# Attention on one core: pairs of key steps with one narrow group each, and maxima over 512 keys

## The reference

```python
h = _sln(hidden, w, ln_g, ln_b, Wg, bg, Wb, bb)
qkv = (h @ Wqkv.T + bqkv).reshape(B, N, num_heads, hd, 3)
...
energy = jnp.einsum('bhqd,bhkd->bhqk', q, k)
att = jax.nn.softmax(energy, axis=-1) / D ** 0.5
out = jnp.einsum('bhqk,bhkd->bhqd', att, v)
```

## Time and profile before

| | us |
|---|---|
| median of 3 runs | 1984.32 (1983.32 to 1984.5) |
| the profiled execution | 1984.56 |
| its span, first to last instruction | 1982.8 |
| TensorE busy | 1898.3 (96%) |
| VectorE busy | 1208.9 (61%) |
| GpSimd busy | 1147.7 (58%) |
| ScalarE busy | 809.0 (41%) |

### The profile page before, as it was taken

The page is one execution under the profiler, slowest core; times in us unless marked ns, Lnnn a source line. Parts: engine busy times, 40 slices in busy tenths (PEclk is TensorE's granted clock), DMA queues, the critical chain, the costliest instruction groups (busy, mean ns, idle before and its releaser), DMA issues. The chain is left out here.

```text
span 1982.8 us, 28225 instructions
## 1 busy us (share of the span) xinstructions
PE 1898.3 (96%) x10520; PEld 1242.2 (63%) x10520; DVE 1208.9 (61%) x1510; ACT 809.0 (41%) x1373; POOL 1147.7 (58%) x589
## 2 busy tenths in 40 slices
PE   6699999999998999998999999999999999999995
PEld 1478888888886888885455555555555555454584
DVE  3556555555646545445766666666666666664289
ACT  1332123122212222211466666666666666666300
POOL 0565565566445121122477777777777777777545
PEclk9899999999999999997899999999999999999997
DMA  6301010100113464566344323444443234405293
GB/s 240 125 1 54 30 56 21 53 32 21 53 40 136 155 215 169 189 197 190 84 98 103 85 78 78 101 108 98 108 103 88 78 78 99 107 24 182 99 391 121
DMA packets 117688, 212.47 MB, mean 107 GB/s; under 512 B 18598, under 2 KB 36134, under 8 KB 117576
## 3 DMA queue, kind: packets, MB, share of 16 engines
q1 hardware_dynamic: 98828, 200.04, 34.1%
q10 hardware_dynamic: 18560, 10.94, 1.9%
q0 software_dynamic: 192, 0.05, 0.0%
HBM read 134.40 MB, written 75.80 MB: 106 GB/s over the span
## 5 line engine op out<-in xcount | busy, mean ns | idle before, releaser
L1371 DVE TENSOR_REDUCE at_mrow<-banks 128x1 f32<-128x1024 f32 x512 | 604.3, 1217 | 270.5 <-PE banks L1204 270.4
L1349 ACT ACTIVATE at_probs<-banks 128x512 f32<-128x512 f32 x1024 | 557.3, 597 | 324.8 <-PE banks L1220 323.7
L1468 POOL TENSOR_TENSOR at_pair<-at_probs 128x2048 f32<-128x2048 f32 x127 | 581.8, 4581 | 170.4 <-ACT at_probs L1349 170.4
L1220 PE MATMUL banks<-early_qs,early_ks 98*128 98x512 f32 x1024 | 442.6, 435 | 5.5 <-ACT at_probs L1349 5.5
L1204 PE MATMUL banks<-early_ks,early_qs 96*128 96x512 f32 x1024 | 375.9, 412 | 6.7 <-PEq L754 3.5
L1220 PEld LDWEIGHTS banks<-early_qs,early_ks 98*128 98x128 f32 x1024 | 191.8, 188 | 211.4 <-ACT at_probs L1349 109.9
L1232 PE MATMUL banks<-at_probs,at_v 128*32 128x512 f32 x2048 | 273.0, 605 | 0.9 <-ACT at_probs L1349 0.9
L1204 PEld LDWEIGHTS banks<-early_ks,early_qs 96*128 96x128 f32 x1024 | 198.2, 196 | 45.3 <-DVE at_mrow L1371 18.8
L67 PE MATMUL banks<-l_ht,l_weights 128*128 128x512 f32 x768 | 179.4, 393 | 5.5 <-ACT l_gt L574 5.5
L67 PE MATMUL banks<-qk_nt,l_weights 128*128 128x512 f32 x768 | 177.2, 392 | 3.0 <-ACT qk_gt L889 3.0
L67 PE MATMUL banks<-l_weights,l_hf 128*128 128x512 f32 x768 | 177.3, 390 | 0.0
(11 more groups left out here) (120 smaller groups left out, 1988.1 us busy)
## 6 DMA issues: line engine op xcount, KB each, us to landing
qk_scratch<-qk_out SPq DMA_DIRECT2D x64, 512.0 KB, 2.8
early_ks<-qk_scratch SPq DMA_DIRECT2D x48, 512.0 KB, 7.0
early_qs<-qk_scratch SPq DMA_DIRECT2D x96, 256.0 KB, 11.6
attn_scratch<-at_out SPq DMA_DIRECT2D x32, 512.0 KB, 2.6
o_a<-attn_scratch SPq DMA_DIRECT2D x32, 512.0 KB, 11.3
v_scratch<-qk_v ACTq DMA_DIRECT2D x32, 256.0 KB, 2.4
at_v<-v_scratch SPq DMA_DIRECT2D x16, 512.0 KB, 14.0
o_x<-x_scratch SPq DMA_DIRECT2D x8, 1024.0 KB, 14.2
```

Of the source, the lines that this page charges most:

```text
L1220: pe.matmul(et[j % 2][:], ks[0:98, slot, j, (i % KC) * P:(i % KC + 1) * P], qs[0:98, slot, i // KC, j, :], start=True, stop=True).then_inc ...
L1349: nc.scalar.activation(probs[:, i % 4, j, :], et[j % 2][:], ACT.Exp).then_inc(exp_done, 1)
L1371: nc.vector.tensor_reduce(mrow[:, half, u:u + 1], e_ps[u % 2], AX.XY, ALU.max).then_inc(max_done, 1)
L1468: nc.gpsimd.tensor_tensor(psum2[:, pair % 2], probs[:, a], probs[:, a + 1], ALU.add).then_inc(pair_ready, 1)
```

## The change

Two steps form a pair, and the pair becomes the unit of every order.

- On TensorE, `FRONT` puts 8 energy products and 8 products for the maxima of a pair into one sequence, then come both `av` and one whole `den`, that of the pair before. At the head of a half `den` stands between the two `av`.
- The banks are dealt out anew: three for energies, three for the maxima, one each for `av` and `den`. Maxima are taken over 512 keys, one bank at a time, so there are twice as many reductions, each half as long. `mrow` has two values per query. `turn_max` turns both with plain products by the identity into the bank of the third product that follows, and VectorE joins them with one more reduction.
- 20 units come before the first step, not 26. `SWITCH` is pair 3, and the turns stand in pairs 2 and 6.
- ScalarE copies `av` and `den` out behind the last exponential of a step, and `den` of the previous group behind step 1 (it was step 3).
- VectorE's reciprocal of the previous group's second half stands behind pair 1, that is step 3 (it was step 5).
- SP spreads those denominators before it stores the first half, and widens the reciprocal before it places the negated maxima.

The diff, cut:

```diff
-        LEAD = 13
-        SWITCH = STEPS - LEAD
-        TURN = (SWITCH + KC + 1, SWITCH + 1)
+        LEAD = 5
+        SWITCH = PAIRS - LEAD
+        TURN = (SWITCH + PAIRS // 2 - 1, SWITCH - 1)
+        SPAN = PAIRS // QH
+        FRONT = ("M", "E") * 6 + ("E", "M", "E", "M")
         PARTS = 2
         DC = CH // PARTS
-        DEN_STEP = KC // 2 - 1
...
-        mrow = sb("at_mrow", [P, QH, UNITS])
+        mrow = sb("at_mrow", [P, QH, 2, UNITS])
...
-        et = sh.ps[0:2]
-        e_ps = [sh.psum[:, 2:4], sh.psum[:, 4:6]]
+        et, em = sh.ps[0:3], sh.ps[3:6]
...
+        def units_of_pair(g, slot, p, with_next):
+            if p >= SWITCH and not with_next:
                 return []
...
-        FIRST_UNITS = 2 * LEAD
+            whose, at = (g + 1, (slot + 1) % RING) if p >= SWITCH else (g, slot)
+            n = 4 * ((p - SWITCH) % PAIRS)
+            return [(whose, at, (n + a) // UNITS, (n + a) % UNITS, keys) for a in range(4) for keys in range(2)]
+        def number(g, half, u, keys):
+            return 2 * (UNITS * (QH * g + half) + u) + keys
+        def turn_bank(g, half):
+            return den_ps if g == 0 and half == 0 else em[(2 * UNITS * halves(g, half) + 2) % 3]
+        FIRST_UNITS = 4 * LEAD
...
+                    spread_den(g - 1, 1)
                     store(g - 1, 0)
-                    spread_den(g - 1, 1)
+                    widen_rden(g - 1, 1)
                 place_neg(g, slot, 1)
+                spread_den(g, 0)
                 if not first:
-                    widen_rden(g - 1, 1)
                     store(g - 1, 1)
-                spread_den(g, 0)
+                widen_rden(g, 0)
                 if with_next:
                     place_neg(g + 1, (slot + 1) % RING, 0)
-                widen_rden(g, 0)
...
-            def max_unit(unit, keys):
...
-                pe.matmul(e_ps[u % 2][:, keys, :], qs[0:96, slot, half, j, c * P:(c + 1) * P],
+            def max_unit(g, slot, half, u, keys):
+                n, j, c = number(g, half, u, keys), u // TT, u % TT
+                if n >= 3:
+                    pe.wait_ge(max_done, n - 2)
+                if n > 2 * UNITS * QH and n % (2 * UNITS) == 2:
+                    pe.wait_ge(negt_taken, n // (2 * UNITS))
+                pe.matmul(em[n % 3][:], qs[0:96, slot, half, j, c * P:(c + 1) * P],
                           ks[0:96, slot, j, keys * CH:(keys + 1) * CH], start=True, stop=True).then_inc(e_done, 1)
             def turn_max(g, half):
-                pe.wait_ge(max_done, UNITS * halves(g, half))
...
-                pe.transpose(den_ps[0:UNITS, 0:P], mrow[:, half], sh.ident[:]).then_inc(mrow_turned, 1)
+                pe.wait_ge(max_done, 2 * UNITS * halves(g, half))
+                for keys in range(2):
+                    last = pe.matmul(turn_bank(g, half)[0:UNITS, keys * P:(keys + 1) * P], mrow[:, half, keys],
+                                     sh.ident[:], start=True, stop=True)
+                last.then_inc(mrow_turned, 1)
             def energies(g, slot, i, j):
...
-                pe.matmul(et[j % 2][:], ks[0:98, slot, j, (i % KC) * P:(i % KC + 1) * P],
+                n = HG * (STEPS * g + i) + j
+                if n >= 3:
+                    pe.wait_ge(exp_done, n - 2)
+                pe.matmul(et[n % 3][:], ks[0:98, slot, j, (i % KC) * P:(i % KC + 1) * P],
                           qs[0:98, slot, i // KC, j, :], start=True, stop=True).then_inc(et_done, 1)
...
-            def den(g, pair, parts, turned=None):
+            def den(g, pair):
                 pe.wait_ge(pair_ready, PAIRS * g + pair + 1)
...
+                n = pair % SPAN
+                if n == 0:
+                    if g == 0 and pair == 0:
+                        pe.wait_ge(negt_taken, 1)
+                    else:
+                        pe.wait_ge(den_taken, QH * g + pair // SPAN)
+                for part in range(PARTS):
                     cols = slice(DC * part, DC * (part + 1))
                     for j in range(HG):
                         last = pe.matmul(den_ps[HD * j:HD * (j + 1), cols], ones_col[:], psum2[:, pair % 2, j, cols],
...
+                                         start=n == 0 and part == 0, stop=n == SPAN - 1 and part == PARTS - 1)
+                last.then_inc(den_done, 1)
+            def den_before(g, p):
+                if p > 0:
+                    den(g, p - 1)
+                elif g > 0:
+                    den(g - 1, PAIRS - 1)
...
             def group(g, slot, nth=None, first=False, load=True, with_next=True):
                 nxt = (slot + 1) % RING
...
-                for i in range(STEPS):
-                    if i % KC == 0:
-                        pe.wait_ge(negm_loaded, 32 * halves(g, i // KC))
-                    if with_next and i == SWITCH:
+                for p in range(PAIRS):
+                    if p % SPAN == 0:
+                        pe.wait_ge(negm_loaded, 32 * halves(g, p // SPAN))
+                    if with_next and p == SWITCH:
                         pe.wait_ge(stack_loaded[nxt], LOADS * (nth + 1))
...
+                    products = iter(units_of_pair(g, slot, p, with_next))
+                    e = 0
+                    for kind in FRONT:
+                        if kind == "E":
+                            energies(g, slot, 2 * p + e // HG, e % HG)
+                            e += 1
+                        else:
+                            for product in islice(products, 1):
                                 max_unit(*product)
...
+                    av(g, slot, 2 * p)
+                    if p % SPAN == 0:
+                        den_before(g, p)
+                        av(g, slot, 2 * p + 1)
+                    else:
+                        av(g, slot, 2 * p + 1)
+                        if p == TURN[1]:
+                            turn_max(g, 1)
+                        if with_next and p == TURN[0]:
+                            turn_max(g + 1, 0)
+                        den_before(g, p)
...
-                        act.wait_ge(et_done, HG * (STEPS * g + i) + j + 1)
-                        nc.scalar.activation(probs[:, i % 4, j, :], et[j % 2][:], ACT.Exp).then_inc(exp_done, 1)
-                        if j == 1 and i == KC:
...
-                        if j == 1 and i == 0 and not first:
...
-                    if i == KC // 2 - 1 and not first:
+                        n = HG * (STEPS * g + i) + j
+                        act.wait_ge(et_done, n + 1)
+                        nc.scalar.activation(probs[:, i % 4, j, :], et[n % 3][:], ACT.Exp).then_inc(exp_done, 1)
+                    if i % KC == KC - 1:
+                        take_av(g, i // KC)
+                    if i == 1 and not first:
                         take_den(g - 1, 1)
-                    if i == KC + KC // 2 - 1:
+                    if i == KC + 1:
                         take_den(g, 0)
...
-            def take_max(g, slot, half, u, n):
-                dve.wait_ge(e_done, 2 * (n + 1))
-                nc.vector.tensor_reduce(mrow[:, half, u:u + 1], e_ps[u % 2], AX.XY, ALU.max).then_inc(max_done, 1)
+            def take_max(g, slot, half, u, keys):
+                n = number(g, half, u, keys)
+                dve.wait_ge(e_done, n + 1)
+                nc.vector.tensor_reduce(mrow[:, half, keys, u:u + 1], em[n % 3][:], AX.X, ALU.max).then_inc(max_done, 1)
             def negate_max(g, half):
+                bank = turn_bank(g, half)
+                joined = bank[0:UNITS, 2 * P:3 * P]
                 dve.wait_ge(mrow_turned, halves(g, half))
...
+                nc.vector.tensor_reduce(joined, bank[0:UNITS, 0:2 * P].rearrange("u (k c) -> u c k", c=P), AX.X, ALU.max).then_inc(maxima_joined, 1)
+                dve.wait_ge(maxima_joined, halves(g, half))
+                if not (g == 0 and half == 0):
                     dve.wait_ge(negm_loaded, 32 * (halves(g, half) - 1))
...
+                nc.vector.tensor_scalar(neg_t[:, HI].bitcast(F32R), joined, -1.0, None, ALU.mult).then_inc(negt_hi, 1)
                 dve.wait_ge(negt_hi, halves(g, half))
...
+                nc.vector.scalar_tensor_tensor(neg_t[:, LO], joined, -1.0, neg_t[:, HI], ALU.mult, ALU.subtract).then_inc(negt_taken, 1)
...
-                for i in range(STEPS):
...
+                for p in range(PAIRS):
+                    for unit in units_of_pair(g, slot, p, with_next):
                         take_max(*unit)
-                    if i == TURN[1]:
+                    if p == TURN[1]:
                         negate_max(g, 1)
-                    if with_next and i == TURN[0]:
+                    if with_next and p == TURN[0]:
                         negate_max(g + 1, 0)
...
-                        take_max(*unit)
-                    if i == DEN_STEP + 2 and not first:
+                    if p == 1 and not first:
                         invert(g - 1, 1)
-                    if i == KC + DEN_STEP + 2:
+                    if p == SPAN + 1:
```

74 lines of the change are left out of this document (6 added, 68 removed).

## The result

The changed kernel takes **2044.72 us** (median of 4 runs, 2042.39 to 2047.47) against 1983.88 for the kernel before on the same chip: a ratio of 1.0304, 95% interval 1.0292 to 1.0316. Its profiled span is 2045.7 us, 62.9 more than before. The forecast was 2033, the range 2003 to 2062.

What follows compares the result with a forecast made beforehand. TensorE and ScalarE were taken to bound each other almost equally. On 1984.56 us, -24.6 - 2.4 + 13.3 - 6 + 49.4 + 7.5 + 11 = +48.2 gave 2033 us, range 2003 to 2062.

Steps and rivals of the forecast that it cites:

- Direction and main cause: Slower, 0.89; VectorE's reciprocal waits 5.4 us for the denominators' spread behind the loads, in groups 1 to 13.
- The pair: Attention pairs with M products take 6.87 us instead of 7.07, for 123 pairs: -24.6 us.
- the rival with longer waits in the pair: Reductions each 0.65 us or later exponentials make a pair 7.07, with the stall as it is: 2057 us; chance 0.14.
- The switch: On TensorE, one way from narrow to wide products and back goes per pair, 0.34 us.
- The turn: Two plain products between AV and den on TensorE, 0.43 us a turn, 31 times: +13.3 us; as the transposition, 0.
- The prologue: Before the first step, 40 products one by one instead of 26 units; first E near 947.5: -6 us (-8 to -3).
- The clock: Half clock after TensorE's idle in pair 2, three chances in four, 0.8 x 14 = +11 us (0 to 30).
- The rival of 2061 us: Clock stays at half longer after each hole, through AV and den of pair 2, 2 us more each; chance 0.08.
- The hole: In pair 2 of groups 1 to 13, AV starts 3.8 us later behind VectorE's wait: +49.4 us (39 to 61).
- Group 15: Same wait behind larger loads, spread landing at about 22, AV at 25.7 instead of 17.9: +7.5 us.
- At no cost: ScalarE's copies of AV and den, GpSimd's additions and the landing of the negated maxima add no time.

Runs made afterwards that it cites:

- the split den: The changed kernel with the reciprocal behind pair 2, plus the first half of each pair's den put behind the twelfth wide product: 2002.49 us.
- the filler's run: The changed kernel with 14 wide products of zeros ahead of the fourth M of pair 2 in groups 1 to 13: 2015.83 us.
- the first experiment's kernel: The changed kernel with the reciprocal of the previous group's second half behind the reductions of pair 2 instead of pair 1: 1960.03 us.
- the transposed turn: The changed kernel with the reciprocal behind pair 2, and the maxima turned by two transpositions instead of two plain products: 1962.47 us.
- the energies-first kernel: The changed kernel with TensorE's order in pair 2 made M and E three times, then five E, then five M: 2048.07 us.

## Why the prediction was right, and its wrong step

**Direction and main cause: right, and shown.** The reciprocal waited once a group in groups 1 to 13 (5.0 to 6.0 us, 5.5 in the mean; forecast 5.4) and not in group 14. The fourth M started 18.5 us after the group's first product, forecast 18.0 + 0.69 = 18.7. Moving the reciprocal, or shrinking the loads, took the loss away.

**The pair: right.** 6.85 us, forecast 6.87; the reduction took 0.68 to 0.69, forecast 0.69; VectorE needed 0.60 us a reduction in a run, forecast 0.61. So the rival with longer waits in the pair fell. The term came out at -27, not -24.6. The switch, 0.34, is borne out by the rows around the split den, 0.33.

**The turn: right,** 0.42 against 0.43 us. That a transposition would be about free was read from the kernel before, and is wrong here: two of them cost as much as two plain products where the turn stands now.

**The prologue: right,** the first E at 947.07, forecast 947.5, and -5.5 us by the first AV set.

**The clock: mis-sized.** The sum had 0.8 us a hole: three chances in four that the clock falls, and 1.0 us over four M and E. It fell every time, and the filler's run and the rows of group 6 give 2.3. The step that failed is that it let the half clock end with the M products. It lasted 6.8 us, 5.2 to 6.1 of them behind the restart: some 1.7 us until AV (4.56 from the fourth M to AV, where the forecast's layout has 2.9), and another 0.6 in AV, which took 2.37 (1333.39 to 1335.76) and not 1.74. The rival of 2061 us had this mechanism (half clock into AV and den), at chance 0.08, and sized it a little too high, 2 us more each where it was 1.5. So the truth lay between forecast and rival, and the weights were wrong. The slow stretch of the earlier trace rows, asked for its length, would not have told: it is 3.4 us long, 641.6 to 645.0. The prologue of attention in the same trace would have. There wide products run one after another from 953.49 on, and yet the clock stays at half for another 5.5 us, into the first AV:

```profile
953.50:959.00 5.50, 5.50 (x16) 3.18 (x18) 3.67 (x4) 3.36 (x6) 0.00 (x0) 0.50 1.04 209
```

The clock's term was 20 us short. The quicker pairs and the smaller hole took 6.6 us off, which is part of why the number was only 12 us low.

**The hole: a little smaller,** 3.5 instead of 3.8 us. **Group 15: about right,** +6.7 against +5.7. Its reciprocal came 20.8 us after the group's first product, forecast 22; its pair took 15.3 us, and the half clock came back twice in the pairs without M, which took 8.08 and 7.84 us; the others took 6.37 to 6.71 (forecast 6.59), and 6.99 with the turn. That these two slow stretches follow from the thin work there was not tested. In the first experiment's kernel, without the hole, all pairs of group 15 took 6.55 to 6.87. But the hole is not needed for them: with the transposed turn the clock fell for 3.4 us there too, where TensorE had idled 1.42 us and no more, and two pairs took 8.05 and 8.01 us.

**At no cost: right in sum.** The copies, GpSimd's additions and the negated maxima show no wait of TensorE in any group between 1100 and 1700 us except the ten of the hole.

## What to carry to other kernels

When a change moves an operation that waits for a small transfer, ask what is queued ahead of that transfer and behind that operation; here 5.5 us of wait a group turned a gain of 1.2% into a loss of 3%. A hole in TensorE was paid twice here, once as itself and again at half clock, and the second part (2.3 us behind 3.5) reached past the products that had waited. When a trace is asked what a slow clock costs, ask it also how far into dense work the half clock reaches. Small operations of VectorE beside long ones of GpSimd should read one operand from on-chip memory, not two.

## What the runs showed of the hardware

- A VectorE operation that reads two operands from on-chip memory was held until GpSimd's addition ended: 4.0 us for 16 columns, and 0.16 with GpSimd idle; a reduction with a single such operand took 0.15 beside the same addition, and an operation with one operand there and one in the banks 0.28. The Trainium skill states this (SBUF — State Buffer, "Who interferes with whom": an instruction of VectorE with two inputs there contends with one of GpSimd that reads there; what they share is an exclusive lock). The traces agree: the join began 0.5 us behind the addition and ended 0.03 us behind it.
- The clock fell in holes of 2.8 to 3.8 us, some 2 us after TensorE's last product. It also fell in the energies-first kernel behind products 0.49 us apart, with 0.99 us of idle in group 6 and no more than 0.31 in group 14. In groups 1 to 13 of both kernels it stayed at half for 6.8 us each time; in groups 14 and 15 there were stretches of 3.4 us. With the hole filled by dense products it did not fall in groups 1 to 13.
- 8 KB behind 3.5 MB on the same queue needed 10.7 us.
- One way from wide to narrow products and back cost 0.33 us around den alone, by the rows of the split den, and 0.34 around AV and den together, by those of the kernel before. Around AV alone it was not measured by itself.
